# A layer with attention and experts: the row maxima as operand rows, the router's exponentials from Tanh, and the first and third expert products on the two halves of the array

## The chip, the cores and the metric

One core of one Trainium2 chip. The time is the device time of one execution in microseconds (us), measured in three runs. The profile is of one execution.

## The reference

The input is 8 x 256 token ids. Three blocks follow each other; C = 64 channels throughout.

```python
# 1. token tower: embedding, 6 layers of causal convolution (3 taps, dilation 2**i), log_softmax
x = einsum('ble,he->bhl', shifted_embedding + channel, in_w) + in_b
for i in range(6):
    h = gelu(causal_conv(x, conv_w[i], conv_b[i], 2 ** i)); h = gelu(pw_w[i] @ h + pw_b[i]); x = x + h
logits = log_softmax(out2_w @ gelu(out1_w @ x))
# 2. linear attention of 8 heads, masked, on s = layernorm(h)
r = einsum('bhtu,bhui->bti', tril(einsum(s, Q, s)), einsum('hij,buj->bhui', E, s))
# 3. a transformer layer on the layernorm of the sum: softmax attention and 8 experts
q, k, v = rope(rmsnorm(x) @ wq.T), rope(... @ wk.T), ... @ wv.T          # 4 query heads, 2 key heads of 16
y = softmax(where(causal, q @ k.T / 4, -1e30)) @ v;  x = x + y @ wo.T
flat = rmsnorm(x)
probs = softmax(flat @ router_w.T);  weights = the 2 largest of 8, normalised
for e in range(8):
    out += weights[:, e] * ((silu(flat @ w1[e].T) * (flat @ w3[e].T)) @ w2[e].T)     # 170 hidden
return x + out
```

The scores reach hundreds, so precision matters: operands are split in a 16 bit part and 16 bit rests, and the products of parts are added up in PSUM. The row maximum is taken off inside the matmuls, as three bf16 parts.

## The kernel before, in words

Every engine has a program of its own, written out by hand in the order in which it runs; only semaphores tie them together. An engine that waits holds up everything that stands behind it in its own program. The 2048 rows are 16 tiles of 128, in 4 pairs of 512 rows (`p`, `n_`) and 8 batches of 256 (`b`).

The stretches of time: the tower (to about 44 us), the linear attention over 16 tiles `g` (to 104 us), the softmax attention over 8 batches `b` (104 to 158 us), the experts (158 to 232 us), and a tail.

**The softmax attention.** `qkT[0:96, g, n, t]` holds queries (n = 0 to 3) and keys (4, 5) of a tile as 6 stacked bf16 parts of 16 channels, so that 96 rows give all products of parts in one matmul. For each batch the scores are computed twice. `scores_for_max` (PE, three thirds `u`) computes them for `third_max` (DVE). `max_split` (DVE) writes the negated maxima as three parts to `nms`, `max_rows` (PE) turns them, and `max_out` (DVE, L1180) copies the turned rows from PSUM to `nmT`. `scores_shifted` (PE) computes the transposed scores and adds the maxima with one further matmul for each head and part of the third, `mm(ov_, selh[:, n_, :], nmT[...])`, where `selh` selects the three rows of a head. `probs` (ACT, L744) is the exponential, `values` (PE) the product with v, `y_rows` (ACT, L751) its copy, `out_rows` (PE) the product with wo, `shares` (DVE, L1192 and L1193) the division by the sums, `head_sum` (POOL, L397 to L399) the sum over the heads and the residual.

PE's order in batch b is: `scores_for_max(b+1, 0)` and `(b+1, 1)`, `values(b-1)`, `scores_for_max(b+1, 2)`, `stack` where one is due, `scores_shifted(b, 0)`, `out_rows(b-1)`, `scores_shifted(b, 1)`, `max_rows(b+1)`, `stack`, `scores_shifted(b, 2)`, `stack`. A `stack(g)` turns the parts `qst` of tile g (PE, L1708) and `stacked(g)` (ACT, L681) copies them to `qkT`. The parts of the last two pairs come from `pair_parts` and `pair_copies` (POOL, L462 to L475). The last pair's rows come late: `second_centre(3)`, `second_bases(3)` (DVE, L1020 to L1033), `second_roots(3)` (POOL, L373), `second_rows(3)` (DVE), `second_split(3)` (POOL, L344 and L345), `rows(3)` (PE, L1677), `h_rows(3)` (ACT), `qkv(3)` (PE), in b = 1 and 2.

**The router's rows.** `rms_square(p)`, `third_root(p)` (POOL, L350), `rms_rows(p)` (DVE, L1210), `third_split(p)` (POOL, L344 and L345: f = high + low in f16), `f_transposed(p)` (PE, L1819), `f_rows` or `router_rows` (ACT or DVE: copy to `fTs`, where rows 0 to 63 are the high part and 64 to 127 the low one), `routed(p)` (PE) and `router_in(p)` (DVE, L1228 and L1229). The exponential of the router's rows is `router_exp` for pairs 0 and 1, and for pairs 2 and 3 a Tanh (`router_tanh`), `eighth_root` (DVE) and three squares (`router_squares`). `ranks` to `gates` (DVE) choose the experts.

**The experts.** 44 steps `u` (11 for each pair: 8 experts and 3 chunks of rests). A step is two groups of two matmuls of 128 rows and 512 columns:

```python
for w_, banks_, read, done in ((w1h, A_BANK, "sil_ready", "a_ps"), (w3h, B_BANK, "hh_ready", "b_ps")):
    ...
    if u >= 2:
        pe.wait_ge(S[read], u - 1)
    for w in range(2):
        r = mm(bank[banks_[u % 2]][:, :], w_[:, w, ORDER[i], :], rhs, w == 0, w == 1)
    r.then_inc(S[done], 1)
```

With both parts of f on the rows, one pass with the weights' high part and one with their low part give all four products. ACT takes the Silu of the first (`sil`, L847), DVE multiplies it with the second (`hh`, L1402), ACT casts that (`high_part`, L827), POOL takes the rest (`low_part`, L415). Between the steps PE runs `down` (groups of w2 products, four or eight of them for a quarter of a chunk, after the steps i = 0, 1, 3, 4, 5, 6, 8 and 9), `sum_up` (i = 5 and 8), and the transposes and router products of the pair after next. DVE weighs and adds their results (`mix`, `weigh_odd`, `add_odd`). The hidden rows stay in a ring of 6 (`RING`), and the two PSUM banks of a group alternate.

## Time and profile before

| what | us |
|---|---|
| median of 3 runs (lowest, highest) | 243.78 (241.18, 245.32) |
| the profiled execution's own time | 241.91 |
| its span | 240.2 |
| PE busy, all matmuls | 203.6 (85%) |
| DVE busy | 176.5 (73%) |
| ACT busy | 152.9 (64%) |
| POOL busy | 145.0 (60%) |
| granted TensorE clock, mean | 0.996 of 2.4 GHz |
| DMA queue of the loads, share of the span | 7.4% |

PE's busy time counts a matmul from its start to its modelled end, which overlaps the next one; the distance between two starts is what a matmul costs. In the lists in order of time a line stands for one or more like instructions ("x2"), the first number is the start of the first, the second the time to the end of the last, and the bracket the engine's idle time before it with what ended it.

### The profile page before, as it was taken

The page shows a single profiled execution, that of the slowest core. Times are in us where ns is not written, and L with a number is a line of the kernel's source. Part 1 is how long each engine was busy: PE and PEld are TensorE (multiplying, and loading weights), DVE is VectorE, ACT ScalarE, POOL GpSimd, SP SyncE. Part 2 cuts the span into 40 slices and gives each one's busy share as a digit, 9 for nine tenths or more (in the row PEclk, how much of TensorE's full clock was granted, in tenths as well). Part 3 has the DMA queues.
Part 4 walks back from the last instruction along what each step waited for, and adds up shares of the span by engine and source line. Part 5 has one row for each costly group of instructions (what it writes and reads, how often), then busy time and mean ns, then how long its engine had stood idle before and what let it go on. Part 6 is the DMA issues. An engine that isn't in the chain of part 4 may idle for free.

```text
span 240.2 us, 7337 instructions
## 1 busy us (share of the span) xinstructions
PE 203.6 (85%) x2836; PEld 134.9 (56%) x2836; DVE 176.5 (73%) x421; ACT 152.9 (64%) x283; POOL 145.0 (60%) x196
## 2 busy tenths in 40 slices
PE   7987788887898998787868979987897969999991
PEld 3653446444565665566646757753464736766671
DVE  3224665959786689978965879667986994899976
ACT  2368867277696677975526555586784766688650
POOL 6840000124588667671678886828886976879671
PEclk9999999999999999999999999999999999999998
DMA  1576410000000000000000000000000010000011
GB/s 37 123 166 137 96 38 3 0 3 0 5 1 3 3 3 3 5 0 3 0 3 0 3 0 3 1 3 1 3 4 0 3 23 0 3 8 17 3 26 23
DMA packets 8398, 4.53 MB, mean 19 GB/s; under 512 B 7556, under 2 KB 7852, under 8 KB 8364
## 3 DMA queue, kind: packets, MB, share of 16 engines
q1 hardware_dynamic: 8364, 4.06, 7.4%
q8 instruction: 23, 0.38, 0.7%
q14 instruction: 11, 0.09, 0.1%
HBM read 3.53 MB, written 0.52 MB: 17 GB/s over the span
## 4 chain that ended last, share of the span: by engine, by line
PE 49%; DVE 21%; ACT 10%; POOL 9%; issue 9%; DVEq 0%; POOLq 0%; ACTq 0%
PE bank L1452 47%; POOL shared L415 2%; DVE nmx L1161 2%; ACT early L681 2%; ACT oT L666 2%; DVE L L1369 1%; POOL stat L373 1%; ACT oTx L672 1%; DVE early L894 1%; PE bank L1708 1%; DVE shared L1001 1%; ACT early L567 1%; DVE shared L1402 1%; DVE nmr L1172 1%; DVE oT L1193 1%
## 5 line engine op out<-in xcount | busy, mean ns | idle before, releaser
L1452 PE MATMUL bank<-early 64*64 64x256 f32 (+5 forms) x556 | 56.4, 351 | 9.7 <-DVE early L894 2.7
L415 POOL TENSOR_TENSOR shared<-shared 128x512 f16<-128x512 f32 x44 | 51.4, 1167 | 15.3 <-ACT shared L827 11.3
L1452 PEld LDWEIGHTS bank<-early 64*64 64x64 f32 (+3 forms) x556 | 30.6, 126 | 27.3 <-ACT early L560 5.2
L1402 DVE SCALAR_TENSOR_TENSOR shared<-bank,qT 128x512 f32<-128x512 f32 x44 | 30.3, 689 | 8.3 <-ACT qT L847 7.4
L847 ACT ACTIVATE qT<-bank 128x512 f32<-128x512 f32 x44 | 26.3, 598 | 12.8 <-PE bank L1452 11.1
L350 POOL TENSOR_TENSOR stat<-stat,neghalf 128x4 f32<-128x4 f32 x8 | 8.2, 1021 | 37.5 <-DVE stat L979 36.2
L827 ACT CAST shared<-shared 128x512 f16<-128x512 f32 x44 | 27.0, 614 | 3.4 <-DVE shared L1402 3.3
L1452 PE MATMUL bank<-onehot,w3h 128*128 128x512 f16 x88 | 26.2, 379 | 1.8 <-DVE shared L1402 1.7
L482 POOL TENSOR_TENSOR oTx<-oT,oTx 128x512 f16<-128x512 f32 x16 | 19.4, 1215 | 12.2 <-ACT oTx L672 12.2
L1452 PE MATMUL bank<-onehot,w1h 128*128 128x512 f16 x88 | 26.2, 380 | 0.4 <-ACT qT L847 0.4
L1452 PE MATMUL bank<-w2xh,shared 128*128 128x128 f16 (+1 forms) x240 | 22.4, 209 | 2.7 <-POOL shared L415 2.4
L1452 PE MATMUL bank<-w2h,shared 128*128 128x64 f16 x384 | 22.7, 193 | 0.0
L1452 PE MATMUL bank<-qT,shared 64*64 64x128 f32 (+1 forms) x320 | 18.5, 326 | 4.9 <-ACT oT L666 2.0
L1161 DVE TENSOR_REDUCE nmx<-bank 128x2 f32<-128x512 f32 (+1 forms) x24 | 16.1, 688 | 7.1 <-PE bank L1452 6.8
L1452 PEld LDWEIGHTS bank<-w2xh,shared 128*128 128x128 f16 x240 | 15.9, 98 | 9.3 <-POOL shared L415 3.5
L894 DVE TENSOR_TENSOR early<-early 128x512 f32<-128x512 f32 x10 | 6.9, 692 | 16.9 <-ACT early L567 16.4
L744 ACT ACTIVATE qT<-bank 128x512 f32<-128x512 f32 x24 | 14.3, 598 | 7.7 <-PE bank L1452 7.6
L1452 PEld LDWEIGHTS bank<-w2h,shared 128*128 128x128 f16 x384 | 18.3, 98 | 0.0
L1452 PEld LDWEIGHTS bank<-qT,shared 64*64 64x64 f32 x320 | 10.8, 132 | 12.1 <-issue 6.8
L666 ACT ACTIVATE oT<-bank 128x512 f32<-128x512 f32 x16 | 9.5, 596 | 10.7 <-PE bank L1452 10.5
L1001 DVE TENSOR_TENSOR shared<-bank,trimul 128x512 f32<-128x512 f32 x16 | 11.0, 688 | 7.0 <-PE bank L1452 5.2
L1452 PEld LDWEIGHTS bank<-onehot,w3h 128*128 128x128 f16 x88 | 8.3, 98 | 13.2 <-DVE shared L1402 4.0
(232 smaller groups left out, 459.9 us busy)
## 6 DMA issues: line engine op xcount, KB each, us to landing
early<-in_tcn_w_dram SPq DMA_DIRECT2D x2, 320.0 KB, 4.1
w1s<-in_w1m_dram SPq DMA_DIRECT2D x2, 256.0 KB, 3.5
qT<-in_w3m_dram SPq DMA_DIRECT2D x2, 256.0 KB, 3.5
out_dram<-L SPq DMA_DIRECT2D x8, 64.0 KB, 1.7
qw<-in_attn_q_dram SPq DMA_DIRECT2D x4, 64.0 KB, 2.4
hTs<-in_w2m_dram SPq DMA_DIRECT2D x1, 256.0 KB
cos<-in_cos_t_dram SPq DMA_DIRECT2D x2, 96.0 KB, 2.2
sin<-in_sin_t_dram SPq DMA_DIRECT2D x2, 96.0 KB, 2.2
```

What stands on the lines that cost most here:

```text
L350: nc.gpsimd.tensor_tensor(stat[:, dst, g4], stat[:, src, g4], neghalf[:, 0:4], ALU.pow) \
L415: nc.gpsimd.tensor_tensor(hhx[:, i, 1, :], hh[:, u % RING, :], hhx[:, i, 0, :], ALU.subtract).then_inc(S["lo_ready"], 1)
L482: nc.gpsimd.tensor_tensor(oTx[:, g % 2, 1, :, :], oT[:, g % 2, :, :], oTx[:, g % 2, 0, :, :], ALU.subtract).then_inc(S["o_low"], 1)
L666: nc.scalar.mul(oT[:, g % 2, :, :].rearrange("p a (cc t) -> p cc a t", cc=2), banks[:, 6:8, 0:256].rearrange("p cc (a t) -> p cc a t", a=4 ...
L744: nc.scalar.activation(pT[:, b % 2, u, :], bank[5 + (3 * b + u) % 2][:, :], ACT.Exp).then_inc(S["exp2_ready"], 1)
L827: nc.scalar.copy(hhx[:, i, 0, :], hh[:, u % RING, :]).then_inc(S["hi_ready"], 1)
L847: nc.scalar.activation(sil[:, u % 2, :], bank[A_BANK[u % 2]][:, :], ACT.Silu, scale=1.0 / FFN_SCALE).then_inc(S["sil_ready"], 1)
L894: V_.tensor_tensor(x_, x_, hid2[:, 2 * s:2 * s + 2, :], ALU.add).then_inc(S["x_ready"], 1)
L1001: V_.tensor_tensor(om[:, g % 2, :].rearrange("p (x j t) -> p x j t", x=2, t=64), banks[:, 4:6, 0:256].rearrange("p x (j t) -> p x j t", t=64),
L1161: V_.tensor_reduce(nmx[:, g, h0:h0 + nh], bank[4 - (3 * b + u) % 2][:, :].rearrange("p (n s) -> p n s", n=nh), AX, ALU.max, negate=True).t ...
L1402: V_.scalar_tensor_tensor(hh[:, u % RING, :], bank[B_BANK[u % 2]][:, :], HH_SCALE / FFN_SCALE, sil[:, u % 2, :], ALU.mult, ALU.mult).then_ ...
L1452: return nc.tensor.matmul(out_, l_, r_, start=a, stop=z, skip_group_check=skip)
```

## The change

Six things change.

- **Maxima as operand rows.** `qkT` gets rows 96 to 107. `max_out(b)` goes from DVE to ACT: it reads the turned maxima from PSUM and writes them, once for the even and once for the odd query heads (2 instructions of 12 rows x 512), beside the queries' parts, multiplied by a column of `headsel`. The keys get ones there (`key_ones`, POOL: 8 copies of 12 x 512, two before the tile loop for each of pairs 0 and 1 and two each in tiles 1 and 2). `selh` and its matmuls go; the K of `scores_shifted` is 108 rows (`K_ROWS`).
- **All router exponentials from Tanh.** `router_exp` goes. Pairs 0 and 1 take one Tanh together in step 1 of the experts, one `eighth_root` in step 2 and three squares in step 3, for `ranks(0)` in step 4.
- **First and third products on the row halves.** The rows of f come from `third_split` as high, high, low, low (128 x 512 for a cast and a subtraction in place of 128 x 256), are turned by 8 transposes in place of 4 and copied as 128 x 1024. `fT2` then holds each part on both halves. A step has six matmuls of 64 rows, alternating between rows 0 to 63 (w1) and 64 to 127 (w3); low times low is left out.
- **The last pair's copies** go from POOL (`pair_copies(3)`) to ACT (`last_copies`, two at a time in b = 3 and 4).
- **Order.** `second_bases(3)` comes before `row_max(2)`; `shares(6)` before `router_in(1)`; `f_transposed(1)` before `scores_shifted(7, 0)`; POOL's `third_root(2)` before the experts, `third_split(2)` from step 4 to 6, `head_sum(7)` from 10 to 8, `third_split(3)` from 20 to 17; `rms_rows(3)` from step 20 to 17, `f_transposed(3)` on PE from 22 to 24, `f_rows(3)` from 23 to 25, `router_in(3)` from 24 to 27.
- `routed` has four products of 64 rows for a tile in place of two of 128.

```diff
+            def key_ones(i):
+                g4 = slice(4 * i, 4 * i + 4)
+                if i == 0:
+                    pool.wait_ge(S["rstd_ready"], 2)
+                    pool.wait_ge(S["q_ps"], 1)
+                for kv in range(NKV):
+                    nc.gpsimd.tensor_copy(qkT[ROW_M:K_ROWS, g4, NH + kv, :], headsel[ROW_M:K_ROWS, kv:kv + 1].unsqueeze(2)
+                                          .to_broadcast([K_ROWS - ROW_M, 4, P])).then_inc(S["ones_ready"], 1)
+                    pool.wait_ge(S["ones_ready"], 2 * i + kv + 1)
...
-                split(shl[:, p % 2, :, :, :], s2[:, p % 2, :, :], "fsplit_ready")
+                d_, src = shf[:, p % 2, :, :, :], s2[:, p % 2, :, :].unsqueeze(2).to_broadcast([P, 4, 2, V])
+                link(nc.gpsimd.tensor_copy(d_[:, :, 0:2, :], src))
+                nc.gpsimd.tensor_tensor(d_[:, :, 2:4, :], src, d_[:, :, 0:2, :], ALU.subtract) \
+                    .then_inc(S["fsplit_ready"], 1)
...
+            def max_out(b):
+
+                act.wait_ge(S["nmT_ps"], b + 1)
+                src = bank[0][ROW_M:K_ROWS, 0:P].bitcast(bf16).rearrange("p (a t) -> p a t", a=2).unsqueeze(2) \
+                    .to_broadcast([K_ROWS - ROW_M, 2, 2, P])
+                for odd in range(2):
+                    r = nc.scalar.mul(qkT[ROW_M:K_ROWS, 2 * b:2 * b + 2, odd:NH:2, :], src,
+                                      headsel[ROW_M:K_ROWS, 2 + odd:3 + odd])
+                r.then_inc(S["nmT_ready"], 1)
+
             h_rows(2)
             second_copies()
+            max_out(0)
             for b in range(B - 1):
                 if b >= 1:
                     y_rows(b - 1)
+                if b == 4:
+                    last_copies(2, 4)
...
                 for u in range(3):
+                    if u == 2 and b == B - 2:
+                        max_out(b + 1)
...
                     probs(b, u)
...
+                    if u == 1 and b == 3:
+                        last_copies(0, 2)
+                    if u == 0 and b == 4:
+                        last_copies(4, 6)
                 if (b, 2) in STACK_B:
                     stacked(STACK_B[b, 2])
+                if b < B - 2:
+                    max_out(b + 1)
...
-            router_exp(0)
-            router_exp(1)
...
                 if u == 1:
                     y_rows(B - 1)
+                    router_tanh(0)
+                if u == 3:
+                    router_squares(0)
...
-                        mm(ov_, qkT[:, 2 * b, NH + n_ // 2, :], qkT[:, 2 * b:2 * b + 2, n_, :], True, False)
-                        mm(ov_, selh[:, n_, :], nmT[:, b % 2, :, :], False, False)
+                        mm(ov_, qkT[0:K_ROWS, 2 * b, NH + n_ // 2, :], qkT[0:K_ROWS, 2 * b:2 * b + 2, n_, :], True,
+                           False)
...
+                a_, b_ = bank[A_BANK[u % 2]][:, :], bank[B_BANK[u % 2]][:, :]
...
+                if u >= 2:
+                    pe.wait_ge(S["sil_ready"], u - 1)
+                mm(a_, w1h[lo_, 0, ORDER[i], :], fT2[n_][lo_, 0, :], True, False)
...
+                if u >= 2:
+                    pe.wait_ge(S["hh_ready"], u - 1)
+                mm(b_, w3h[hi_, 0, ORDER[i], :], fT2[n_][hi_, 0, :], True, False)
+                mm(a_, w1h[lo_, 1, ORDER[i], :], fT2[n_][lo_, 0, :], False, False)
+                mm(b_, w3h[hi_, 1, ORDER[i], :], fT2[n_][hi_, 0, :], False, False)
+                mm(a_, w1h[lo_, 0, ORDER[i], :], fT2[n_][lo_, 1, :], False, True).then_inc(S["a_ps"], 1)
+                mm(b_, w3h[hi_, 0, ORDER[i], :], fT2[n_][hi_, 1, :], False, True).then_inc(S["b_ps"], 1)
```

## Rows read from the trace of the kernel before

**Rows 1.** Busy us (instructions) by stretch: PE, PEld, DVE, ACT, POOL; then granted clock, DMA

```profile
104.00:158.00 54.00, 44.90 (x581) 33.80 (x582) 40.68 (x116) 29.42 (x55) 37.72 (x68) 1.00 0.01 2
158.00:199.00 41.00, 33.33 (x381) 19.74 (x380) 34.38 (x79) 27.75 (x53) 32.42 (x34) 1.00 0.02 5
199.00:231.70 32.70, 32.70 (x422) 22.38 (x420) 27.17 (x62) 23.80 (x46) 24.08 (x22) 1.00 0.03 6
```

**Rows 2.** In order of time, PE: matmuls of one expert step

```profile
214.99 0.59 PE L1452 MATMUL bank<-onehot,w1h 128*128 128x512 f16 x2
215.42 0.59 PE L1452 MATMUL bank<-onehot,w3h 128*128 128x512 f16 x2
215.85 0.33 PE L1452 MATMUL bank<-w2xh,shared 128*128 128x128 f16 x3
```

**Rows 3.** Matmuls in order of time: where the array changes its tiling, three places

```profile
71.28 0.60 PE L1452 MATMUL bank<-sTs,qwh 128*128 128x512 f16 x2
71.80 0.53 PE L1452 MATMUL bank<-qT,shared 64*64 64x128 f32 x6
...
116.27 0.22 PE L1452 MATMUL bank<-mask_s,identb 128*128 128x128 bf16 x1
116.41 0.38 PE L1452 MATMUL bank<-wo_sb,yT 64*128 64x130 f32 x2
...
116.74 0.39 PE L1452 MATMUL bank<-wo_sb,yT 64*128 64x130 f32 x4
117.06 0.28 PE L1452 MATMUL bank<-early 96*128 96x256 bf16 x1
```

**Rows 4.** Order of time on DVE, PE and ACT where the attention ends

```profile
157.79 0.19 DVE L1228 TENSOR_REDUCE stat<-bank 128x4 f32<-128x32 f32 x1 [2.66 <-PE bank L1452]
...
159.45 0.88 PE L1452 MATMUL bank<-qT,vaug 128*32 128x256 f32 x16 [0.81 <-DVE oT L1193]
...
158.49 1.28 ACT L847 ACT_TABLE_LOAD   x1
```

**Rows 5.** Order of time on DVE and PE in the expert stretch: idle times in brackets

```profile
181.09 0.42 DVE L1200 TENSOR_TENSOR sqr<-idx 128x256 f32<-128x256 f32 x1 [1.75 <-POOL idx L399]
...
195.28 0.59 PE L1452 MATMUL bank<-onehot,w3h 128*128 128x512 f16 x2
198.68 0.40 PE L1819 MATMUL bank<-ident,shl 128*128 128x128 f16 x4 [2.80 <-POOL shl L345]
```

**Rows 6.** Order of time, 112 to 140 us: what the last pair of rows waits for

```profile
112.88 0.55 DVE L1069 TENSOR_TENSOR rope<-bank,rot 128x384 f32<-128x384 f32 x1
...
119.20 1.64 POOL L373 TENSOR_TENSOR stat<-stat,neghalf 128x8 f32<-128x8 f32 x1 [1.98 <-DVE stat L1033]
...
123.02 0.40 PE L1677 MATMUL bank<-ident,shlB 128*128 128x128 f16 x4 [1.84 <-POOL shlB L345]
...
139.47 0.54 PE L1708 MATMUL bank<-identb,qst 128*96 128x128 bf16 x6 [0.58 <-POOL qst L475]
```

**Rows 7.** Order of time on ACT and DVE: the first maxima

```profile
106.28 1.64 ACT L792 COPY qst<-qst 128x256 bf16<-128x256 bf16 x6
107.78 0.27 DVE L1180 COPY nmT<-bank 128x256 bf16<-128x256 bf16 x1
```

**Rows 8.** Groups of a line and shape: busy us, mean ns | idle before, releasers

```profile
L1452 PE MATMUL bank<-nmT,selh 128*128 128x256 bf16 x32 | 8.7, 273 | 0.0
...
L744 ACT ACTIVATE qT<-bank 128x512 f32<-128x512 f32 x24 | 14.3, 598 | 7.7 <-PE bank L1452 7.6
L681 ACT COPY early<-bank 96x768 bf16<-96x768 bf16 x16 | 12.5, 793 | 3.8 <-PE bank L1708 3.6
...
L415 POOL TENSOR_TENSOR shared<-shared 128x512 f16<-128x512 f32 x44 | 51.4, 1167 | 15.3 <-ACT shared L827 11.3 <-issue 1.7 <-DVE s L1210 0.8
L345 POOL TENSOR_TENSOR shl<-s,shl 128x256 f16<-128x256 f32 x4 | 2.7, 671 | 0.3
L344 POOL CAST shl<-s 128x256 f16<-128x256 f32 x4 | 1.6, 397 | 1.7 <-DVE s L1210 1.6
```

More of the change, by code:

```diff
@@ L78, in tower @@
         mask_s = sb("mask_s", [P, 4, P], bf16)
-        selh = sb("selh", [P, NH, P], bf16)
+        headsel = sb("headsel", [P, 4])
         neghalf = sb("neghalf", [P, 4])
@@ L422, in _ @@
             variance_root(1)
+            key_ones(0)
+            key_ones(1)
             def last_rotary():
@@ L491, in _ @@
                     first_split(1)
+                if g in (1, 2):
+                    key_ones(g + 1)
                 if g == 2:
@@ L792, in second_copies, with last_copies @@
                     nc.scalar.copy(d_[:, :, heads, dst, :], d_[:, :, heads, src, :]).then_inc(S["copies1_ready"], 1)
+            def last_copies(first, last):
+                d_ = qst[:, 1, :, :, :, :]
+                q_, k_ = slice(0, 4), slice(4, 6)
+                for heads, dst, src, parts in ((q_, 1, 0, 1), (q_, 2, 0, 1), (k_, 3, 0, 1), (k_, 5, 0, 1), (q_, 4, 3, 3),
+                                               (k_, 4, 1, 4))[first:last]:
+                    act.wait_ge(S["parts3_ready"], parts)
+                    nc.scalar.copy(d_[:, :, heads, dst, :], d_[:, :, heads, src, :]).then_inc(S["copies3_ready"], 1)
+            def max_out(b):
[6 more added lines that the diff above has]
+                r.then_inc(S["nmT_ready"], 1)
             h_rows(2)
             second_copies()
+            max_out(0)
             for b in range(B - 1):
@@ L1289, in _ @@
             max_split(1)
-            rotary_products(2)
-            max_out(1)
-            rotary_sums(2)
+            rotary(2)
             second_centre(3)
+            second_bases(3)
             for b in range(1, B):
@@ L1302, in _ @@
                     router_rows(1, 1)
-                    router_in(1)
                 if b >= 1:
                     shares(b - 1)
-                if b + 1 < B:
-                    max_out(b + 1)
+                if b == 7:
+                    router_in(1)
                 if b == 6:
@@ L1817, in f_transposed @@
                     pe.wait_ge(S["fin_ready"], 2)
-                for a in range(4):
-                    r = nc.tensor.transpose(bank[b_][:, 64 * a:64 * a + 64].bitcast(f16),
-                                            shl[:, p % 2, a, :, :].rearrange("p a b -> p (a b)"), ident16[:, :])
+                for x_ in range(2):
+                    for a in range(4):
+                        r = nc.tensor.transpose(bank[b_][:, 256 * x_ + 64 * a:256 * x_ + 64 * a + 64].bitcast(f16),
+                                                shf[:, p % 2, a, 2 * x_:2 * x_ + 2, :].rearrange("p a b -> p (a b)"),
+                                                ident16[:, :])
                 r.then_inc(S["trf_ps"], 1)
@@ L1902, in _ @@
                 values(b - 1)
+                if b == 1:
+                    scores_shifted(1, 0)
                 if b == 2:
```

200 lines of the change are left out of this document (99 added, 101 removed).

## Prediction, written before the changed kernel was run

> **What bounds the kernel now.** I read the page's engine shares first (PE 85%, DVE 73%, DMA 7.4%: no transfer is late after the first 45 us), then the chain of waits (most of it matmuls), then the stretches. In the last of the three expert stretches PE is busy for all of its 32.7 us and waits for nothing; in the one before it is busy for 33.3 of 41.0, beside DVE with 34.4; in the attention 44.9 of 54.0 [rows 1]. The clock is at its full level in all three, so no cost below comes from it. So PE is the bound of the later half of the experts, PE and DVE share the first half, and in the attention PE is the busiest of four engines that wait for each other. The tail after 231.7 us and everything before 104 us are touched only in passing.
>
> **Part 1: six products of half height.** Today a step's four matmuls start 0.216 us apart, 0.86 us from step to step where nothing lies between [rows 2]. Six matmuls in three concurrent pairs would be 3 x 0.216 = 0.65, so 0.21 saved, 9.2 us for 44 steps. That pairs do run together is shown for f32: two matmuls on different row halves end within 0.38 us, where one f32 matmul of that group takes nearly that by itself [rows 3]. For f16, which streams a column each cycle in place of one in two, no row shows it; I take full overlap and keep none as a rival.
>
> The price is the change of tiling. From a 512-column matmul of 128 rows to one of 64: the second of two starts at 71.28 + 0.22, its columns end at 71.71, the next starts at 71.80, so 0.09 is lost; from a 128-column one, 116.27 to 116.41 is 0.14 where 0.055 are columns, 0.09 again. Back: the pairs from 116.74 are 0.11 apart, the second ends its columns at 116.96, the next group starts at 117.06, 0.10 [rows 3]. So 0.093 each way. PE leaves the step's tiling for `down` and the rest after 8 of 11 steps of pairs 1 to 3 (9 in pair 2) and 6 of pair 0: 31 round trips and some singles, 63 x 0.093 = 5.9 us. So 64% of the gain on paper goes back. Net for PE: 9.2 - 5.9 = 3.3 us, or 0.8 for a pair's 17.5 us. The doubled transposes (4 more of 0.055) and router products (8 more of 0.025) cost 0.4 for each of pairs 2 and 3.
>
> The Trainium skill, TensorEngine Tiling (Array Packing), section Key Properties, says that changing the tiling mode, not only the tile, drains the engine; the trace agrees, with the 0.093 us above. It gives no price. It is the rule that speaks against this change.
>
> A step also waits for both banks at its start, where `w3` used to wait 0.43 later. From the end of a step its Silu (0.6), `hh` (0.69) and hand-overs need about 1.6 until that bank is free; with no `down` between two of the three steps PE is back after 0.65 + 0.9 = 1.55. Five places of 11 are like that, and cost 0 to 0.3 us each. So for pairs 2 and 3, PE's own half, I count -0.8 together (0.8 x 2, half of it given back), with bounds of -1.6 and +1.5. In pairs 0 and 1 DVE and POOL cover the gain: DVE works without a gap for most of it, and POOL's rest costs 1.17 a step against PE's 0.65 [rows 8]. There I count nothing.
>
> **Part 2: what the new order frees.** (a) PE stands idle for 2.8 us before the transposes of the last rows, since POOL's split of them comes late [rows 5]; some 0.5 of it other waits would have taken. Rows and split now come three steps earlier and the transposes two later: five steps of 1.55 against a split that grows from 0.40 + 0.67 to about 0.65 + 1.17 = 1.8 [rows 8]. The stall goes: -2.2 (bounds -2.8, -1.5). (b) DVE stands for 1.75 us before the square of the last rows, which need `head_sum(7)` [rows 5]; that comes two steps earlier, and nothing else on DVE is late there: -1.8 with what follows (bounds -2.3, 0, since POOL's earlier split is 0.7 longer). (c) At the hand-over DVE waits 2.66 us in `router_in(1)` with `shares(6)` behind it, and PE 0.81 for those; ACT loads its table after `router_exp` for 1.28 us until 159.77 [rows 4]. Both go, and next is DVE's own work before the first `hh`: -0.7 (bounds -1.3, 0). (d) Against that, ACT now waits in step 3 for `eighth_root(0)`, which stands behind `shares(7)` on DVE, and the Silu of step 3, the cast of step 2 and the first `down` stand behind it: 1.1 of shares + 0.7 + three squares of 0.23 against the 0.9 that the pipeline has there: +0.8 (bounds 0, +1.6).
>
> **Part 3: the attention.** The 64 matmuls with `selh` go [rows 8]. At 0.108 for 256 columns and 0.055 for 128 (the step of 512 columns scaled) that is 32 x 0.163 = 5.2 us of PE, 0.65 a batch; the 12 more rows of K cost nothing, as a matmul takes its columns. But the maxima's own chain comes next: from the end of `scores_for_max(b+1, 2)` to `max_rows(b+1)` DVE needs about 1.95 us (0.2 to its start, a reduction of 0.69, four small operations), and what PE does meanwhile shrinks from 1.9 to 1.4. So of 0.65 a batch I count 0.2 in the five regular ones, -1.0.
>
> ACT gets two instructions of 12 x 512 for each batch. The nearest rows are 128 x 512 at 0.598 and 96 x 768 at 0.793 [rows 8]; I take 0.6 each, 1.2 a batch, between 0.8 and 1.6. That is 9.6 us more on an engine that is busy for 29.4 of 54.0 [rows 1]. Where it lies: after `probs(b, 2)` and before `y_rows(b)`, and PE meanwhile has `values(b)` (0.9) and `scores_for_max(b+2, 2)` (0.35), so it is hidden to within 0.1 in most batches. Not so the first: the copies end at 107.92 and `max_out(0)` at 109.1, in place of 108.05 [rows 7], so the first shifted scores come 0.8 later: +0.5 after what `selh` gives back. And in batch 6 it stands ahead of `probs(6, 2)`, and `f_transposed(1)`, whose split is 0.7 longer, stands ahead of `scores_shifted(7, 0)`: +0.4.
>
> The rows of the last pair are a chain of their own, on which PE stands idle for 1.84 us until 123.02: bases on DVE behind `row_max(2)`, root on POOL at 119.20, rows, split, transposes [rows 6]. The bases now come before `row_max(2)`, and without `max_out(1)` ahead of it the rotary sum of 112.88 [rows 6] comes 0.8 earlier, and so POOL's parts before the root. The root starts at about 116.5; then `row_max(2)` and `shares(0)` end at 119.5 and are the later condition of `second_rows(3)`, which ran at 120.87. So -1.4 (bounds -2, 0). The copies of the last pair on ACT end before `stack(12)` asks, which waited 0.58 [rows 6], but with more for ACT at that place: -0.5, and -0.4 where POOL has 2.1 us less before the router's first rows. Sum for the attention: -1.0 + 0.5 + 0.4 - 1.4 - 0.5 - 0.4 = -2.4 (bounds -5, +2).
>
> `key_ones` puts 8 copies of up to 0.65 us on POOL. The first four run after the second root, at 51.2 to 53.8, where POOL idled until 53.54; the others after `low_rows` of tiles 0 and 1, with over 1 us of idle time each. If that cover were gone it would be 2.6 us; I count 0. `headsel` replaces `selh` where POOL idles ahead of 44 us: 0.
>
> **Sum.** -2.4 (attention) - 0.7 + 0.8 (hand-over, step 3) - 1.8 - 2.2 (the two stalls) - 0.8 (products) = -7.1 us: span 240.2 to 233.1, the execution 241.91 to 234.8. The runs' median is 1.9 above the profiled time, so 243.78 - 7.1 = 236.7.
>
> **Rivals.** R1, the halves overlap only partly in f16, so that six cost about what four cost today (0.86 [rows 2]) in place of 0.65: PE gains nothing on a step and pays the tilings, 1.5 a pair in its own half and part of it before. Against the forecast +0.8 + 2 x 1.5 + 1: about 241.5. For it: two streams of a column each cycle into PSUM are shown by no row; against it: the f32 pairs lose only 0.007. The Trainium skill, TensorE: Matmul & The Clock Gate, section Measured speedup vs the span model, has four row tiles of 512 columns at 3.07 times one, 77% of ideal; by that rule a step would be 0.84, nearly R1's.
>
> R2, the other side: the halves take turns. Six matmuls are then 1.30 us, +0.43 a step and the tilings: 11 x 0.43 + 1.5 = 6.2 for a pair; pairs 2 and 3 pay it whole (+12.4), pairs 0 and 1 some half (+6). With the rest as forecast (-6.3 without the products): 243.8 + 18.4 - 6.3, about 256. It decides from a step of about 0.95.
>
> R3, ACT becomes the attention's bound: its work in a batch with two `stacked` is 1.8 + 0.37 + 1.6 + 1.2 = 5.0 us in program order, against batches of 5.5 to 7.3 now. If `max_out` isn't covered, each of 7 batches waits up to 0.8 for it: +5.6 against the forecast, 242.3. For it: ACT's waits are short in the batches with two copies; against it: 24 us idle in 54.
>
> R4, the stalls go but new ones come in their place in pairs 0 and 1, where DVE had no gaps: (a) and (b) give 1.5 and not 4.0: 239.2. This is the low end of the forecast's own case, for the most part.
>
> R5, the change of order works better, since PE's stalls of pairs 0 and 1 (33.3 of 41.0 busy) go as well: 2 to 4 us more, about 233.
>
> **How the numbers follow.** A measurement of this kernel can hardly tell less than 2% (4.9 us) from no change. Chances: forecast (234.5 to 238.9) 0.43; R5 0.12; R4 0.16, half of it within 2%; R3 0.13; R1 0.11; R2 0.05. The range is 231.5 to 243.5: it takes in R1, R3, R4 and most of R5 and leaves out R2 and the edges. Faster by over 2% (under 238.9): 0.43 + 0.12 + 0.08 and a little of R3, 0.65; within 2%: 0.26; slower: R2 and the worst of R1 and R3, where a cover fails besides, 0.09.
>
> **What would show it.** The w1h and w3h groups as 64*128, six to a step, pairs starting under 0.01 us apart and steps without `down` 0.65 apart in PE's half (0.84: R1; 1.30: R2). 0.09 us at each change of tiling. No idle PE before the transposes of step 24; DVE without the 1.75 at the square of the last rows. `max_out` at 0.5 to 0.7 for each of its 16 instructions; yT's copy right behind it without PE idle before `out_rows`. The rows' transposes at about 121.7 in place of 123.02. A batch should take about 0.2 less, and pair 3 of the experts about 17 us. I am wrong if ACT stands ahead of PE's shifted scores in most batches, or if two streams into PSUM slow each other.

## The result, and the profile after

The changed kernel takes 247.71 us (median of 4 runs, 247.38 to 249.39) against 243.14 for the kernel before (4 runs, 241.18 to 245.32): ratio 1.022, 95% interval 1.017 to 1.028. I forecast 236.7, range 231.5 to 243.5. The profiled execution took 247.72 us, span 245.6; that of the kernel before 241.91 and 240.2. Its granted clock is 0.967 in the mean, in place of 0.996.

The same three stretches as in [rows 1], the last one cut where the experts end now. Columns: length, busy time (instructions) of PE, PEld, DVE, ACT, POOL, then granted clock, DMA share, GB/s.

```profile
104.00:158.00 54.00, 44.83 (x550) 31.40 (x547) 41.55 (x111) 42.61 (x78) 37.34 (x62) 0.94 0.01 2
158.00:199.00 41.00, 33.94 (x450) 19.64 (x452) 33.27 (x78) 27.52 (x56) 33.01 (x33) 0.96 0.01 3
199.00:237.00 38.00, 34.57 (x463) 21.22 (x460) 28.71 (x65) 23.90 (x47) 24.89 (x23) 0.96 0.03 7
```

The last stretch, which PE filled without a gap before (32.7 us), is now 38.0 long with PE busy for 34.57. And the clock is below full in all three. The stretches of 2 us that hold most of the loss:

```profile
110.00:112.00 2.00, 1.69 (x13) 1.28 (x11) 1.79 (x8) 1.47 (x3) 0.00 (x0) 0.50 0.00 0
...
168.00:170.00 2.00, 1.68 (x20) 1.43 (x22) 1.90 (x5) 0.73 (x2) 1.84 (x3) 0.50 0.01 4
...
208.00:210.00 2.00, 1.43 (x4) 1.16 (x5) 0.45 (x3) 0.23 (x1) 0.74 (x1) 0.69 0.00 0
210.00:212.00 2.00, 2.00 (x22) 1.48 (x22) 0.00 (x0) 0.00 (x0) 0.00 (x0) 0.50 0.00 0
```

0.50 is the level of 1.2 GHz. What comes ahead of each of the three, in order of time on ACT, PE and DVE (idle time before an instruction and its releaser in brackets):

```profile
108.36 1.25 ACT L836 ACTIVATE early<-bank,headsel 12x512 bf16<-12x512 bf16 x2
109.67 0.32 PE L1502 MATMUL bank<-early 108*128 108x256 bf16 x1 [0.75 <-ACT early L836]
...
164.63 0.22 DVE L1290 SCALAR_TENSOR_TENSOR lg<-lg,bank 128x64 f32<-128x64 f32 x1
164.88 0.54 ACT L802 ACTIVATE lg<-lg 128x64 f32<-128x64 f32 x2 [2.33 <-DVE lg L1290]
166.25 0.39 PE L1502 MATMUL bank<-onehot,w1h 64*128 64x512 f16 x1 [2.61 <-ACT qT L905]
...
207.38 0.69 DVE L1381 TENSOR_TENSOR bank<-bank,gate 128x512 f32<-128x512 f32 x1
208.33 0.19 DVE L1281 TENSOR_TENSOR lg<-bank,stat 128x32 f32<-128x32 f32 x1
208.57 1.92 PE L1502 MATMUL bank<-qst,identf 128*128 128x256 f32 x4 [2.67 <-DVE lg L1281]
212.78 0.60 ACT L905 ACTIVATE qT<-bank 128x512 f32<-128x512 f32 x1 [4.00 <-PE bank L1502]
```

Each wait is read from the bottom up. PE's 2.61 is Silu's lateness; Silu stands behind `router_squares(0)`, which waits for `eighth_root(0)` on DVE (L1288 to L1290), which stands behind `shares(7)`. PE's 2.67 is `sum_up(1, 0)` waiting for `router_in(3)`, which the change moved from step 24 to step 27 on DVE, where it stands behind `hh(27)` and `weigh_odd` (L1381); `sum_up(1, 0)` stands in the same step on PE. Behind it PE finds itself at the half clock, and ACT is idle for 4.00.

The row halves themselves run as forecast; PE, in order of time (answers to [rows 2, 3]):

```profile
203.16 0.39 PE L1502 MATMUL bank<-sTs,w1h 64*128 64x512 f16 x1
203.16 0.39 PE L1502 MATMUL bank<-sTs,w3h 64*128 64x512 f16 x1
203.39 0.38 PE L1502 MATMUL bank<-sTs,w1h 64*128 64x512 f16 x1
203.39 0.38 PE L1502 MATMUL bank<-sTs,w3h 64*128 64x512 f16 x1
203.60 0.38 PE L1502 MATMUL bank<-sTs,w1h 64*128 64x512 f16 x1
...
203.82 0.34 PE L1502 MATMUL bank<-rwh,sTs 64*128 64x8 f16 x8
```

Two products start together, 0.22 apart from the next two, 0.66 a set (203.16 to 203.82). And the stalls that were to go are gone (answers to [rows 5] and, for 122.63, [rows 6], whose idle time was 1.84), in order of time:

```profile
181.37 0.42 DVE L1252 TENSOR_TENSOR sqr<-idx 128x256 f32<-128x256 f32 x1
...
201.06 0.62 PE L1873 MATMUL bank<-ident,shared 128*128 128x128 f16 x8
...
122.63 0.40 PE L1727 MATMUL bank<-ident,shlB 128*128 128x128 f16 x4 [0.20 <-POOL shlB L362]
```

Two new groups, `max_out` on ACT and the doubled split on POOL (answers to [rows 8]):

```profile
L836 ACT ACTIVATE early<-bank,headsel 12x512 bf16<-12x512 bf16 x16 | 10.0, 671 | 0.3
L421 POOL TENSOR_TENSOR shared<-s,shared 128x512 f16<-128x512 f32 x3 | 3.5, 1155 | 0.2
```

For the experiments I read one more number from each trace: the time from the start of `hh(0)` to that of `hh(43)`, the first and the last of the 44 instructions of that kind on DVE; stretches between other `hh` are read in the same way. It is 71.7 us before (160.41 to 232.12) and 77.5 after (160.06 to 237.57): all of the loss lies in these 44 steps.

### The profile page after: what moved, and what is told of

The parts are those of the page before. It is cut to its first block, busy times and chain, and to the rows that moved or that the text cites. A ratio compares the mean times of both kernels' runs of the same rounds, so it can differ in the third digit from the quotient of the medians.

```text
span 245.6 us, 7505 instructions
## 1 busy us (share of the span) xinstructions
PE 205.9 (84%) x2908; PEld 131.2 (53%) x2908; DVE 179.7 (73%) x416; ACT 165.6 (67%) x307; POOL 150.8 (61%) x203
## 4 chain that ended last, share of the span: by engine, by line
PE 48%; DVE 22%; ACT 13%; issue 8%; POOL 7%; DVEq 0%; POOLq 0%; ACTq 0%
PE bank L1502 44%; POOL shared L446 3%; DVE shared L1450 3%; ACT early L714 2%; PE bank L1761 2%; ACT qT L905 2%; ACT oT L699 1%; DVE nmx L1219 1%; DVE L L1417 1%; ACT oTx L705 1%; DVE early L952 1%; ACT early L600 1%; DVE shared L1059 1%; DVE oT L1245 1%; ACT early L836 1%
## 5 line engine op out<-in xcount | busy, mean ns | idle before, releaser
L1502 PE MATMUL bank<-early 64*64 64x256 f32 (+7 forms) x556 | 55.3, 357 | 10.1 <-DVE early L952 2.7
L1502 PEld LDWEIGHTS bank<-early 64*64 64x64 f32 (+4 forms) x556 | 30.9, 129 | 29.1 <-issue 6.1
L1450 DVE SCALAR_TENSOR_TENSOR shared<-bank,qT 128x512 f32<-128x512 f32 x44 | 30.2, 689 | 15.4 <-ACT qT L905 14.4
L1502 PE MATMUL bank<-w2xh,shared 128*128 128x128 f16 (+1 forms) x240 | 23.4, 214 | 3.3 <-POOL shared L446 2.8
L1502 PE MATMUL bank<-w2h,shared 128*128 128x64 f16 x384 | 23.4, 196 | 0.0
L1502 PEld LDWEIGHTS bank<-w2xh,shared 128*128 128x128 f16 x240 | 14.8, 100 | 14.2 <-POOL shared L446 8.6
L1219 DVE TENSOR_REDUCE nmx<-bank 128x2 f32<-128x512 f32 (+1 forms) x24 | 16.1, 687 | 7.6 <-PE bank L1502 7.2
L1502 PE MATMUL bank<-onehot,w1h 64*128 64x512 f16 x66 | 18.4, 390 | 2.6 <-ACT qT L905 2.6
L1502 PE MATMUL bank<-sTs,w3h 64*128 64x512 f16 x66 | 18.0, 383 | 1.7 <-DVE shared L1450 1.7
L1502 PEld LDWEIGHTS bank<-w2h,shared 128*128 128x128 f16 x384 | 19.1, 100 | 0.0
L1502 PE MATMUL bank<-onehot,w3h 64*128 64x512 f16 x66 | 18.1, 390 | 0.9 <-DVE shared L1450 0.9
L1502 PE MATMUL bank<-sTs,w1h 64*128 64x512 f16 x66 | 18.0, 383 | 0.0
```

The costliest lines, as they stand in the source:

```text
L1219: V_.tensor_reduce(nmx[:, g, h0:h0 + nh], bank[4 - (3 * b + u) % 2][:, :].rearrange("p (n s) -> p n s", n=nh), AX, ALU.max, negate=True).t ...
L1450: V_.scalar_tensor_tensor(hh[:, u % RING, :], bank[B_BANK[u % 2]][:, :], HH_SCALE / FFN_SCALE, sil[:, u % 2, :], ALU.mult, ALU.mult).then_ ...
L1502: return nc.tensor.matmul(out_, l_, r_, start=a, stop=z, skip_group_check=skip)
```

## Experiments

Ratios are against the kernel before on the same chip; "steps" is hh(0) to hh(43) of the profiled run. The rows were measured in several rounds, in which the kernel before itself had medians of 242.6 to 243.8, and an interval is 0.3 to 1.1% to each side; so differences of under some 2 us between two rows are only as good as the marks in the traces that go with them.

| kernel | median us (runs) | ratio, 95% interval | steps us |
|---|---|---|---|
| after | 247.71 (4) | 1.022, 1.017 to 1.028 | 77.5 |
| a1_rin25 | 245.38 (4) | 1.011, 1.003 to 1.018 | 74.0 |
| a2_sq5 | 245.16 (4) | 1.013, 1.005 to 1.020 | 76.0 |
| a3_both | 242.07 (4) | 0.998, 0.990 to 1.005 | 71.7 |
| a4_fill | 243.32 (4) | 1.001, 0.994 to 1.008 | 71.4 |
| b1_skew | 239.32 (8) | 0.988, 0.984 to 0.992 | 70.4 |
| b2_ft1 | 240.50 (5) | 0.993, 0.990 to 0.996 | 71.6 |
| b3_prod | 236.73 (4) | 0.977, 0.973 to 0.981 | 67.7 |
| b4_maxundo | 243.42 (10) | 1.004, 1.001 to 1.007 | 70.4 |
| c1_best | 236.01 (4) | 0.974, 0.967 to 0.981 | 67.7 |
| c2_afterprod | 242.65 (10) | 0.999, 0.995 to 1.002 | 73.2 |
| c3_prep | 238.37 (4) | 0.985, 0.978 to 0.991 | 68.5 |
| c4_halves | 252.48 (4) | | 80.7 |
| d1_ahead | 237.68 (4) | 0.979, 0.971 to 0.986 | 69.0 |
| d2_couple | 240.51 (4) | 0.989, 0.981 to 0.997 | 69.6 |
| d3_tile | 242.95 (10) | 1.004, 0.999 to 1.008 | 73.3 |
| d4_skewft | 238.80 (4) | 0.982, 0.973 to 0.991 | 69.3 |
| e1_maxearly | 236.21 (4) | 0.973, 0.962 to 0.984 | 67.7 |
| e2_fill | 235.82 (4) | 0.968, 0.960 to 0.976 | 67.7 |

### The two router steps

```diff
-                if u == 27:                       # a1_rin25, DVE
+                if u == 25:
                     router_in(3)
-                if u == 3:                        # a2_sq5, ACT
+                if u == 5:
                     router_squares(0)
-        GATE_STEPS = ((4, 5, 6, 7), ...
+        GATE_STEPS = ((5, 6, 6, 7), ...
```

a3_both has both, a4_fill also three products on PE in the wait of the first `scores_shifted` (their lines stand under the last experiments).

> The changed kernel with one edit: VectorE runs the last pair's router_in(3) two steps earlier (step 25, not 27). Theory W (the waits): the changed kernel loses its time in a few idles of TensorE, each followed by a stretch at the half clock. The largest is at 208.57, where sum_up(1, 0) waits 2.67 us for VectorE's step 27 with router_in(3) in it; the granted clock then is 0.50 in 210 to 212, and hh(28) comes 4.5 us later against the kernel before than hh(27) does. W gives 247.7 - 4.5 = about 243.2 (242.5 to 244.5), and no 0.50 behind step 27. Rival H (the row halves: tiling changes and the new order of the six products cost a little in each of the 44 steps): nothing but the 2.67 of the wait itself can go, and what is saved is lost again in the steps after it, 245 to 247. Rival A (ScalarE has become the bound by its added max_out): 247, the wait moves to another place.

> The changed kernel with one edit: ScalarE's router_squares(0) at step 5, not step 3, and pair 0's ranks at step 5, not 4, so that ScalarE no longer waits (2.33 us at 164.88) for VectorE's eighth_root(0), and TensorE no longer waits 2.61 us for Silu at 166.25. W: the stretch of 0.50 in 168 to 170 goes; but the marks behind it (hh(13) +0.3 to +0.4, hh(22) +2.3, hh(23) -0.4 against before) say that the 1.8 us lost there are mostly given back by step 14, so 246.2 to 247.7. H and A: 247 to 248.

> Both edits of a1_rin25 and a2_sq5. W: 241.5 to 243.5, both stretches at the half clock inside the 44 steps gone, and the mean granted clock up from 0.967 to about 0.985. H: 245 to 247. A: 246 to 247.

> a3_both, and TensorE, while it waits for max_out(0) on ScalarE in front of the first scores_shifted (109.67, a wait of 0.75 us that follows a thin stretch), makes three 128x512 products into a bank that is written anew right after, so that it has no idle there. The output is the same. W, if the fall of the granted clock to 0.50 in 110 to 116 comes of TensorE's thin work before it: the clock stays at 1.0 there, and values(0), max_rows(2), values(1) (+2.5, +2.0, +1.3 against before) come 1 to 2 us earlier; of this little is left at the end, since rows(3) is at -0.3 already with the low clock: -0.3 to -1.0 against a3_both. H and A: no difference from a3_both.

Measured against the changed kernel: -2.3, -2.5 and, both together, -5.6 us. So W holds for the sum, and the steps are back at 71.7. It was wrong on the shares: a1 gave half of its 4.5, as its profile had the clock at 0.50 in 168 to 172 as well, and a2 gave more than the marks behind it promised. H had given 245 to 247 for a3, A 246 to 247: neither is the cause of these 5.6. W was also wrong on the clock: both long waits are gone in a3_both, and yet its clock falls inside the 44 steps (length, busy times, granted clock as above):

```profile
166.00:168.00 2.00, 1.38 (x7) 0.43 (x8) 1.50 (x3) 1.34 (x5) 0.85 (x2) 0.71 0.00 0
168.00:170.00 2.00, 2.00 (x22) 1.39 (x22) 1.21 (x3) 0.94 (x2) 1.43 (x2) 0.50 0.01 4
```

The traces give the shares more closely than the medians do. From hh(22) to hh(33) it is 22.3 us with `router_in(3)` at step 27 and 18.0 with it at step 25, in both pairs of kernels that differ in it: 4.3 for a wait of 2.67, with the half clock behind it. (Without row halves, c2_afterprod against b3_prod below, the same stretch loses 2.7 for a wait of 2.4, and the clock stays full.) From hh(0) to hh(3) it is 6.2 with the squares at step 3 and 4.7 with them at step 5: 1.5 for a wait of 2.61.

a4_fill can't be told from a3_both; a3_both's own profile had no fall of the clock at 110, so this pair said nothing on it (e2_fill, below).

### The parts: products, maxima, place of the transposes

```diff
+            # b1_skew: one set is A(u+1) beside B(u)
+                pe.wait_ge(S["sil_ready"], u)
+                pe.wait_ge(S["hh_ready"], u - 1)
+                for w in range(3):
+                    first_products(u + 1, w)      # w1h, rows 0 to 63
+                    r = mm(b_, w3h[hi_, ...], fT2[n_][hi_, ...], w == 0, w == 2)
             # b2_ft1
-            f_transposed(1, 1)
             scores_shifted(B - 1, 0)
+            f_transposed(1, 1)
             # b3_prod: fTs, shl split, 4 transposes, two 128-row products each for w1h, w3h, as before
             # b4_maxundo: selh, nmT, max_out on DVE, as before
```

> a3_both with one edit: TensorE pairs the first products of step u+1 with the third products of step u (A(0) alone ahead of the loop), in place of both of step u. Theory K (coupling): in a3_both a set of six products starts only when hh(u-2) has read its bank, and Silu(u) waits for the whole set, where in the kernel before the two first products of a step ran ahead of that wait; the trace has TensorE waiting 0.97 us for VectorE at 219.39 and ScalarE idle 0.27 to 0.44 ahead of each Silu there. hh(28) to hh(43) took 24.2 us in a3_both and 23.1 in the kernel before, though its PE work is less. K gives 22.5 to 23.4 for that stretch, 1 to 2 less over the 44 steps as a whole: 239.5 to 241.3 in all. Rival V (VectorE, busy 20.9 of those 24.2 us, is the bound, and its idle time only moves): 241.7 to 242.5, the stretch at 23.9 to 24.3.

> a3_both with one edit: f_transposed(1) behind scores_shifted(7, 0) again, as in the kernel before, not ahead of it. In a3_both TensorE waits 1.24 us for GpSimd's third split at 153.16, all of attention's last scores behind it, and its clock is at 0.50 in 154 to 156. If that wait counts: 0.6 to 1.2 less, 240.9 to 241.5, and no 0.50 there. If the hand-over is set by the last values and VectorE's router work instead: 241.8 to 242.3.

> a3_both with the products part undone: two 128-row products each for w1 and w3 on one copy of the rows (fTs), the split in 64-element halves and the 128x512 copies of the kernel before; maxima, router and the order of the rest as in a3_both. By my forecast's terms (0.65 us for six products against 0.86 for four, less 63 changes of tiling at 0.093) this costs 0.8: 242.9. K: the four products of before let Silu run ahead, so it is 0.3 to 1.2 faster than a3_both: 240.9 to 241.8. V: 241.8 to 242.5.

> a3_both with the maxima part undone: selh and nmT again, max_out a 128x256 copy on VectorE, the extra product per head in scores_shifted, no key_ones. By my forecast's attention terms (selh 1.0, less max_out's 0.5 and 0.4) this costs about 0.1 to 1.0: 242.2 to 243.1. Rival A (ScalarE's added 2 x 0.62 us for each of eight maxima, and the wait for max_out(0), cost more than the 48 products save): 240.5 to 241.8, with max_rows(2) at 117.6 as in the kernel before and not at 119.4.

b3_prod is the finding: with everything else of the change kept, taking the row halves out gives 5.3 us, where my term had them worth 0.8. Its result lies below what any of the theories in its expectation allowed. b4_maxundo is 1.4 slower than a3_both, with intervals that overlap; in its trace hh(0) comes at 162.8, in those of a3_both and a2_sq5 at 161.2 and 159.1. Both speak for a gain by the maxima part and against rival A, which had b4_maxundo faster than a3_both. b2_ft1 took 1.6, again with intervals that overlap. In a3_both the wait for POOL's longer split read (PE, in order of time)

```profile
153.16 1.03 PE L1873 MATMUL bank<-ident,shared 128*128 128x128 f16 x8 [1.24 <-POOL shared L421]
```

and the clock was at 0.50 in 154 to 156 behind it. But a2_sq5 and c3_prep have the same wait of 1.24 us and the full clock behind it, and hh(0) comes at 159.12 in a2_sq5, at 159.07 in b2_ft1. So what b2_ft1 saves is, by these traces, the stretch at the half clock where an execution has one, and not the wait.

b1_skew took 2.8 in the median (its 8 runs spread over 238.4 to 242.0; 1.3 in the steps of the profiled one). The trace of a3_both shows what it undoes, PE and DVE in order of time:

```profile
218.64 0.69 DVE L1450 SCALAR_TENSOR_TENSOR shared<-bank,qT 128x512 f32<-128x512 f32 x1
...
219.39 0.39 PE L1502 MATMUL bank<-sTs,w3h 64*128 64x512 f16 x1 [0.48 <-DVE shared L1450]
219.40 0.39 PE L1502 MATMUL bank<-sTs,w1h 64*128 64x512 f16 x1
```

The `w1h` product at 219.40 needs nothing of that `hh`, but it stands in one set with `w3h`, which needs its bank. In the kernel before, `w1h` could run ahead. This counts most in step 5; PE and DVE, the kernel before:

```profile
164.48 0.59 PE L1452 MATMUL bank<-onehot,w1h 128*128 128x512 f16 x2
164.86 0.68 DVE L1402 SCALAR_TENSOR_TENSOR shared<-bank,qT 128x512 f32<-128x512 f32 x1
165.59 0.60 PE L1452 MATMUL bank<-onehot,w3h 128*128 128x512 f16 x2 [0.52 <-DVE shared L1402]
```

The two `w1h` products were made before `w3h` had its bank. The same step in a3_both:

```profile
166.62 0.41 PE L1502 MATMUL bank<-onehot,w3h 64*128 64x512 f16 x1 [1.87 <-DVE shared L1450]
166.62 0.41 PE L1502 MATMUL bank<-onehot,w1h 64*128 64x512 f16 x1
```

In b1_skew the stretch hh(28) to hh(43) went from 24.1 only to 23.5, just short of K's 22.5 to 23.4.

### Is it the preparation, the coupling or the tiling

```diff
             # c3_prep: a3_both, but four products in the order of before
+                    for w in range(2):
+                        r = mm(bank[...], w_[:, w, ORDER[i], :], fT2[n_][:, w, :], w == 0, w == 1)
             # d2_couple: c3_prep's products in a set's order
+                mm(a_, w1h[:, 0, ...]); pe.wait_ge(S["hh_ready"], u - 1)
+                mm(b_, w3h[:, 0, ...]); mm(a_, w1h[:, 1, ...]); mm(b_, w3h[:, 1, ...])
             # d3_tile: c3_prep's last product of a step on rows 64 to 127
+                        rows_ = hi_ if w_ is w3h and w else slice(0, P)
             # d1_ahead: c1_best, with the w1h products of step u+1 ahead of w3h's of step u
             # c1_best: b3_prod + b2_ft1; d4_skewft: b1_skew + b2_ft1
```

> b3_prod and b2_ft1 together: a3_both with the products part undone and f_transposed(1) behind scores_shifted(7, 0). b2_ft1 took 1.6 off a3_both, mostly as one PE wait (1.24 us) and a stretch at the half clock behind it; b3_prod has four transposes there and shows no such wait, so nothing of the 1.6 is left to win: 236.3 to 237.2. If the place of f_transposed counts by itself: 235.2 to 236.

> The changed kernel with its products part undone and nothing else: router_in(3) at step 27 and router_squares(0) at step 3 as the change has them. If the two misplaced router steps cost what they cost in the changed kernel (a1_rin25, a2_sq5, a3_both: 5.6 together), 236.7 + 5.6 = 242.3. If they cost that much only because the sets of six products leave no slack: 238 to 240. Without the part the forecast's other terms remain (7.1 - 0.8 = 6.3 off 242.6), 236.3 by my forecast.

> a3_both with only the inner order of the first products as before: for each step two 128-row products for w1, then two for w3, on fT2's rows as they lie; the doubled split, transposes, copies and router products of the change stay. The products then sum other parts than the reference's, so that the output differs; the amount of work is that of b3_prod's products with a3_both's preparation. Theory K (coupling of the two first products in one set) puts most of the 5.3 between a3_both and b3_prod there: 237 to 238.5. Rival P (the doubled preparation: GpSimd's split of 1.8 us for 1.1, twice in the 44 steps, eight transposes for four, copies of 1.0 us for 0.6): 240 to 242.

> The kernel before with the products part alone (doubled split, transposes and copies, sets of six products on row halves; maxima, router and every place in the order as before). By my forecast's term: 0.8 less, 241.8, if the longer split (0.7 more ahead of f_transposed(3), for which TensorE waits 2.80 at 198.68) is hidden, 242.5 if not. K with P, from a3_both against b3_prod: 4 to 5.5 more, 246.5 to 248.

> c1_best with one edit: TensorE makes the two first products (w1, 128 rows) of step u+1 ahead of the two third products (w3) of step u, so that they don't stand behind the wait for hh(u-2). If waits of the chain TensorE, Silu, hh still cost in c1_best (VectorE waited 4.7 us for Silu in the 44 steps of b3_prod, ScalarE 7.8 us for TensorE): 0.5 to 2 less, 234.0 to 235.5. Rival V (VectorE's own work is the bound there): 235.7 to 236.5.

> c3_prep with one edit: its four 128-row products of a step stand in the order of the changed kernel's sets (w1, then the wait for hh(u-2), w3, w1, w3), so that Silu(u) waits for hh(u-2) and the whole set, with no row halves and no change of tiling. The output is as little the reference's as c3_prep's. Theory K (coupling): most of the 3.7 between c3_prep and a3_both comes back, 240.5 to 242. Theory T (the changes between 64-row and 128-row tiling): nothing comes back, 238.2 to 238.8.

> c3_prep with one edit: the last product of each step (w3, second part) runs on rows 64 to 127 alone, its other half left out, so that every step has two changes of tiling and nothing is coupled. 88 changes by 0.093 are 8.2 us of TensorE's time. T: they are on the path where TensorE is short of slack, 240 to 242. K: TensorE has slack between its waits, and they cost 0 to 1: 238.2 to 239.4.

> b1_skew and b2_ft1 together: the changed kernel with all its parts, the two router steps moved, w1 of step u+1 paired with w3 of step u, and f_transposed(1) behind scores_shifted(7, 0). If the two gains add (2.8 and 1.6 off 242.1): 237.7. If they are in part the same stretch at the half clock: 238.5 to 239.3.

c2_afterprod: 242.65, as the first case said. The misplaced router steps cost 5.9 without row halves and 5.6 with them; the row halves 5.1 with the steps misplaced and 5.3 without (in the steps of the traces 5.6 and 5.9, and 4.3 and 4.0). The two losses add.

c3_prep: 238.4, in K's range. It, d2_couple and d3_tile sum other parts than the reference, so they are compared for their time alone. The doubled preparation is 1.6 of the 5.3, and most of that is the late start: hh(0) comes 1.2 later than in b3_prod, and 1.0 later in b2_ft1, which has no wait at 153. The sets are the other 3.7 (3.1 in the steps).

d2_couple and d3_tile both cost, so neither K nor T holds alone. Coupling alone: +2.1 in the median, on intervals that overlap, and 1.1 in the steps. Two changes of tiling a step, 88 in all: +4.6 (4.7 in the steps), of 8.2 us of PE's time. How the coupling works shows in what Silu waited for, in the 44 steps of c3_prep, d2_couple and d3_tile (us in total, times, longest):

```profile
ACT qT L905 <- PE bank L1502: 8.2, 13, 1.2
```

```profile
ACT qT L905 <- PE bank L1502: 11.9, 17, 1.3
```

```profile
ACT qT L905 <- PE bank L1502: 17.0, 20, 1.6
```

The clock has a share in the 3.1 as well. b4_maxundo makes the same sets, but its clock stayed full through the 44 steps: hh(3) to hh(8) took 8.2 there and in c3_prep, and 9.7 in a3_both with its low clock. Its steps took 70.4, those of c3_prep 68.5. So of the 3.1 about 1.3 came with the low clock and 1.8 with the sets at the full clock, and 1.1 of the 1.8 is what d2_couple has for the order alone. The last ten steps, hh(33) to hh(43), with no low clock in any of these, say the same: 15.1 before, 15.4 in b3_prod and c3_prep, 15.8 in d2_couple, 16.1 in the changed kernel, a3_both and b4_maxundo, and 15.5 in b1_skew.

The change of tiling, d3_tile, PEld and PE in order of time:

```profile
218.05 0.70 PE L1502 MATMUL bank<-sTs,w3h 128*128 128x512 f16 x2
218.36 0.09 PEld L1502 LDWEIGHTS bank<-sTs,w3h 64*128 64x128 f16 x1 [0.42 <-issue]
218.68 0.17 PEld L1502 LDWEIGHTS bank<-w2xh,shared 128*128 128x128 f16 x3 [0.23 <-issue]
218.68 0.34 PE L1502 MATMUL bank<-w2xh,shared 128*128 128x128 f16 x3
```

The weights of the first product after a change start with it, at 218.36 and 218.68, 0.31 and 0.32 after the product before, which streams for 0.216: 0.095 and 0.10 for each change.

c4_halves, the row halves alone in the order of before, is the dearest: 248.0 at its fastest (its runs differ more than others, 248.0 to 253.2, so no ratio is given), 4.4 over the 243.62 measured beside it, at the upper end of what K with P had given. The profile is of an execution of 251.8 us, so it shows where that one waited and not what the 4.4 are made of. Where the row halves meet the old place of the last split, PE waits longer than the 2.80 of [rows 5], and DVE behind it:

```profile
205.07 1.03 PE L1826 MATMUL bank<-ident,shared 128*128 128x128 f16 x8 [3.54 <-POOL shared L396]
...
209.44 0.69 DVE L1408 SCALAR_TENSOR_TENSOR shared<-bank,qT 128x512 f32<-128x512 f32 x1 [5.47 <-ACT qT L853]
```

c1_best is faster than both kernels: 236.01, ratio 0.974, on the edge between its two cases and not to be told from b3_prod. d4_skewft, the whole change with its placing mended, is faster than before too (0.982) but some 2.8 slower than c1_best; it fell in its second case, so the two gains overlap. d1_ahead was meant to help c1_best and cost 1.7 (1.3 in the steps), which neither theory had: PE then waited 3.4 us for Silu at the next step's `w1h`, with `w3h` behind it, and the cast of `hh` on ACT 14.4 us for DVE in place of 6.8. Of an order of two products on one in-order engine, each choice puts one of them behind the other's wait.

### The start of the attention

Both on c1_best:

```diff
             # e1_maxearly, ACT, in second_copies
+                    if parts == 3:
+                        max_out(0)
             # e2_fill (and a4_fill), PE, scores_shifted(0, 0)
+                    for _i in range(3):
+                        mm(bank[5][:, :], identb[:, :], mask_t[...], True, True)
                 pe.wait_ge(S["nmT_ready"], b + 1)
```

> c1_best with one edit: ScalarE's max_out(0) ahead of the last two of the six second_copies, so that it begins at about 107.5 and not at 107.84, and TensorE's wait at 109.14 (0.76) shrinks by 0.4. If attention's start sets what follows: 0.3 to 0.6 less, 235.4 to 235.8. If stack(4) (which waits for those copies) or ScalarE's next steps take it back, as rows(3) at 122 to 123 in every version suggests: 235.8 to 236.3.

> c1_best with the three 128x512 products of a4_fill in TensorE's wait for max_out(0). In c1_best the granted clock was 0.50 in 112 to 114 and 0.66 in 114 to 116, behind that wait. If the idle is what brings the fall: the clock stays at 1.00 to 116, values(0) comes at about 113.4 and not at 114.83. What is left of it at the end: nothing measurable if attention's later steps absorb it (values(1) at 121.1 to 121.5 in all versions, low clock or not), 235.7 to 236.3; 0.5 to 1.0 less if not.

Nothing measurable in either. In e2_fill the clock stayed at 1.00 to 116 and values(0) came at 113.1 and not 114.6; then it fell in 118 to 120, behind another thin stretch:

```profile
118.00:120.00 2.00, 1.98 (x16) 1.57 (x16) 1.83 (x9) 1.12 (x3) 0.00 (x0) 0.50 0.00 0
```

By max_rows(7) both kernels are level, 150.0 in c1_best and 150.2 in e2_fill. As the low stretch only moved, this pair alone doesn't price it. But a4_fill has no low clock anywhere in the attention, and its hh(0) comes at 159.8, no earlier than that of a2_sq5 (159.1), which has 0.50 to 0.89 in 110 to 116. So no run shows that the low clock at the attention's start costs anything at its end.

## Why the prediction was wrong

Forecast -7.1, measured +4.6 (+5.8 in the profiled executions). In the time itself the miss is 11.0 us, as the kernel before came out 0.6 lower than the 243.78 that I started from: waits of 5.6 that I had at 0.8 make 4.8 of it, and row halves of 5.3 that I had at -0.8 make 6.1. The term that failed by most is the one of the products.

- **Step 3, term (d), +0.8 (0 to 1.6): mis-sized.** The chain was the right one, but its own terms, 1.1 + 0.7 + 0.7 - 0.9, give 1.6, and I entered half of that. The root took 1.07 and the squares 0.84, and PE waited 2.61. a2_sq5 puts the term at 2.5 in the median and at 1.5 in the steps. The half clock behind the wait can't be put down to it: a2_sq5, without the wait, has 0.50 in 166 to 168.
- **router_in(3): the step that failed most plainly.** I said of the new order only that stalls go. A step moved later on DVE must be followed to each of its waiters: `f_transposed(3)` and `routed(3)` were moved with it, `sum_up(1, 0)` on PE was not, and it waits for the same count. I had no term for it; it costs 2.3 alone and 3.1 once step 3 is mended, and 4.3 in its own stretch of the traces. R4 was near it in kind (new stalls in place of the old ones), but had 2.5 us and named no place.
- **Part 1, products, -0.8 (-1.6 to +1.5): wrong, +5.3.** Full overlap was right, R1 and R2 are out: the Trainium skill's 3.07 for four row tiles (TensorE: Matmul & The Clock Gate, Measured speedup vs the span model) isn't what two tiles do here, 0.22 for a pair and 0.216 for one. The price of the tiling was right too, 0.095 against my 0.093. What failed is the sentence on the wait for both banks, "Five places of 11 are like that, and cost 0 to 0.3 us each". The 0.8 that the sum gives back is no more than the doubled transposes and router products of two pairs (0.4 each), so nothing of it was left for these waits: d2_couple has 2.1 for that order alone (1.1 in the steps), and in the last ten steps the sets cost 0.7 where I had a gain. And in pairs 0 and 1 I counted nothing "where DVE and POOL cover the gain": they covered the gain and not the cost. The doubled preparation before the last scores, which I had inside a +0.4, makes hh(0) 1.2 later (c3_prep against b3_prod).
- **(a) -2.2 and (b) -1.8: right, as far as the trace shows** (no run has them alone). hh(22) to hh(23) went from 3.87 to 1.20, hh(12) to hh(13) from 3.81 to 2.00.
- **Attention and hand-over, -2.4 and -0.7: right in size where nothing else disturbs.** In b3_prod hh(0) stands 2.3 earlier than before, in c1_best 2.5, in the changed kernel 0.35. Of its parts, the -1.4 for the last pair's rows was too large: their transposes came at 122.63 (122.11 in b3_prod) and not at the 121.7 that I had given. R3 is out: undoing the maxima doesn't gain, and `probs` on ACT still waited 2.6 us for PE in the attention; `max_out` took 0.67 for each of its instructions against my 0.6.
- **The whole without the two failed steps:** -7.1 + 0.8 (products) - 0.8 (step 3) gives 236.7; b3_prod has neither and took 236.73. The agreement to a tenth is luck: the kernel before had 242.58 beside it and not 243.78, so the gain was 5.9 against the forecast's 7.1. The size isn't luck.
- **The clock**, at its full level in all rows of before, I kept out of the sum. In the changed kernel each of the two long waits is followed by some 4 us at 0.50 to 0.70. The fall at 208 went with its wait; the one at 166 did not, and costs 1.3 in the steps of a3_both.

Left open: how the sets' 3.7 in the median divide in full. In the traces the order has 1.1 and the low clock 1.3; the 0.7 that is left would be what the changes of tiling cost over the 0.21 that a step saves; no run has that alone. And what brings the fall at 166 stays open: behind a wait of 1.9 us in step 5 the clock fell in a3_both and not in b4_maxundo.

## What to carry to other kernels

Two products that used to wait for different banks become one when they are put side by side: the earlier one inherits the later one's wait, and everything that lived off its head start pays. When a step is moved on one engine, follow every semaphore it raises to every waiter that wasn't moved with it, and count in that more than the wait may be lost: here 2.67 us on a dense TensorE, with the half clock behind it, became 4.3, and 2.4 us with the full clock behind it 2.7. A change of several parts can hold a gain (here 2.6%) that one of its parts hides.

## What the runs showed of the hardware

- Two f16 matmuls of 64 rows and 512 columns on different row halves run in the time of one, 0.22 us (203.16, 203.39, 203.60), against 0.216 for one of 128 rows ([rows 2]).
- A change between 64-row and 128-row tiling costs 0.095 to 0.10 us each way, and the next product's weights load when it starts and not ahead of it (218.36, 218.68 in d3_tile). By the Trainium skill, TensorEngine Tiling (Array Packing), Key Properties, a change of mode drains the engine; the trace agrees.
- The granted clock went to its level of 1.2 GHz after PE's idles of 2.61 and 2.67 us, and once after 0.75 in a thin stretch, but not after the 2.80 of [rows 5] in the kernel before. After the same idle of 1.24 us it fell in a3_both (0.50 in 154 to 156) and not in c3_prep, and after one of 1.9 us in a3_both and not in b4_maxundo. Which idle brings the fall these runs don't tell.
